# Own tile for the squares of Q, and the head's projections in another order, in a fused attention and mixing kernel

## Chip, cores and metric

The kernel runs as one program on all 8 cores of a Trainium2 chip. Each core works on two of the 16 sequences, and nothing is exchanged between cores. The metric is the device time of the slowest core, in microseconds (us); a median of runs is given. The profile shows one execution on its slowest core, core 4.

## What is computed

For every sequence x of 2048 tokens by 2048 features:

```
x = x + attn(layernorm(x)) @ Wo
x = x + layernorm(x) @ (sum of 8 factors / sqrt(8)) + bias

attn:  q = rmsnorm(h @ Wqa) @ Wqb          16 heads, each 128 (nope) + 64 (rope)
       ckv, k_pe = split(h @ Wkva)         512 + 64, k_pe shared by all heads
       k_nope, v = rmsnorm(ckv) @ Wkvb     16 heads, each 128 + 128
       rope on q_pe and k_pe
       softmax(causal(q k^T / sqrt(192))) v, per head
```

The softmax here isn't shifted by the true maximum of a row but by a bound on it, the product of the norm of the row's q and the largest norm of a k. For that bound the kernel needs, for every head, the squares of Q and K, the maximum of K's squares and the sums of Q's squares per token.

## The kernel before

A core treats its two sequences one after the other (`_emit_seq`). In each there are these stages: layer norm and the two low-rank projections by tiles of 128 tokens; the rope part of q for all heads; the 16 heads; the output projection with the second layer norm; the mixing matrix. The change lies in the heads, and there in what stands between two of them.

All engines have an order written out by hand: the program emits instructions engine by engine in the order of the Python code, each with the semaphores it waits for (`waits`) and the one that it raises (`inc`). ACT, DVE and the DMA queues go through theirs in that order.

A head's body is a loop over 16 tiles of keys. PE multiplies K with Q into psB (L897, and L902 for the 64 rope rows with two rows of statistics added), ACT takes the exponential (L914), DVE masks the diagonal (L921), PE multiplies with V into psA (L934) and sums the columns with small matmuls against a column of ones (L948). In between, ACT scales the next head's weights. When the body has ended, DVE copies psA out (L957) and takes the reciprocal of the sums (L963), which PE transposes (L966) and two small DMAs lay flat.

Between two heads three things follow:

- `prep` projects the next head in 16 groups of matmuls, each into one of six banks (psA 0 to 3, psB 2 and 3, in turn), and each followed by its eviction. `bn_group` makes Q (12 matmuls of 512 columns a group, L661; ACT evicts to QnT, L668), `c1_group` makes K (4 of 512, L678; ACT evicts to KnT, L685), `c2_group` makes V (16 of 128 columns, L698; DVE evicts to Vh, L706), `tq_group` transposes the rope part of q (4, L717; DVE evicts to QpeT_aug, L723). A group waits for the eviction of the group that had its bank before.
- PE spreads the reciprocals over all partitions (L997 to L1017), and ACT copies them out in two halves (L1007, L1024).
- `emit_mhat` makes the bound for the next head. ACT squares K into sq_all (L769), DVE takes the maximum along the tokens (L773) and casts it (L776). ACT then squares Q into the same tile sq_all (L779) and the rope part into sq_pe (L783). PE sums K's maximum (L789, L793) and then Q's squares in 32 matmuls of one column (L803, L808), and L813 spreads the K part. ACT and DVE make the square root of the product (L797, L817 to L828). In the first head of a sequence DVE also makes the maximum of the shared rope key first (L760 to L766).

Then DVE scales the head's output (L1033), makes the two rows of statistics (L843, L846), PE transposes them (L850), and two DMAs of 4 KB put them under QpeT_aug (L856, L859), which L902 waits for.

In the first sequence GpSimd also adds up the eight factors beside the heads (`emit_f_build`), with transfers of 1 MB (L221 to L230).

The tiles of this stage lie one behind the other in SBUF; sq_all takes 4 KiB of each partition.

Of the kernel before, what the change touches and what calls it, by code (L numbers as in the profile page):

```python
# [10 lines left out]
BF16 = mybir.dt.bfloat16  # L11
AF = mybir.ActivationFunctionType
# [3 lines left out]
S = 2048  # L16
# [69 lines left out]
def build_nc():  # L86
# [39 lines left out]
    ones_col = sb("ones_col", [128, 1], BF16)  # L126
# [53 lines left out]
    c_mq = ch("mq"); c_mt = ch("mt"); c_mv = ch("mv"); c_sg = ch("sg")  # L180
# [5 lines left out]
    for fn in [  # L186
# [26 lines left out]
      waits=[(c_bld, 16)], inc=c_bias)  # L213
# [29 lines left out]
    def rsb(name, shape, dt):  # L243
        _uid[0] += 1
        return rctx[0].enter_context(
            nc.sbuf_tensor(f"{name}_u{_uid[0]}", shape, dt, side="right"))
# [7 lines left out]
    def _emit_seq(sq):  # L254
# [47 lines left out]
        for tt in range(NT):  # L302
# [36 lines left out]
              waits=lw, inc=c_ln1)  # L339
# [228 lines left out]
        stage_w = rsb("stage_w", [128, 1536], F32)  # L568
        sq_all = rsb("sq_all", [128, S], BF16)
        sq_pe = rsb("sq_pe", [64, S], BF16)  # L570
        kpesq = rsb("kpesq", [64, S], BF16)
        neg_mh = rsb("neg_mh", [128, 32], F32)
        stat_sa = rsb("stat_sa", [128, 32], F32)
# [78 lines left out]
        def prep(h, pb0, pb1):  # L652
# [5 lines left out]
            def bn_group(cci):  # L658
                def g(bps, boff, waits):
                    for kb in range(12):  # L660
                        E("tensor", lambda e, kb=kb, cci=cci, bps=bps, boff=boff: e.matmul(  # L661
                            out=bps[:, boff:boff + 512],
                            lhsT=wqbn_h[hb][:, kb * 128:(kb + 1) * 128],
                            rhs=qa_v()[:, kb, cci * 512:(cci + 1) * 512],
                            start=(kb == 0), stop=(kb == 11)),
                          waits=(waits if kb == 0 else []),
                          inc=(c_bn if kb == 11 else None))
                    E("scalar", lambda e, cci=cci, bps=bps, boff=boff: e.activation(  # L668
                        out=QnT[hb][:, cci * 512:(cci + 1) * 512],
                        in_=bps[:, boff:boff + 512], func=AF.Copy),  # L670
                      waits=[(c_bn, c_bn.n)], inc=c_bn_ev)
                    return (c_bn_ev, c_bn_ev.n)
                return g, [whf_mark]

            def c1_group(cci):
                def g(bps, boff, waits):
                    for kb in range(4):
                        E("tensor", lambda e, kb=kb, cci=cci, bps=bps, boff=boff: e.matmul(  # L678
                            out=bps[:, boff:boff + 512],
                            lhsT=wkvbk_h[hb][:, kb * 128:(kb + 1) * 128],  # L680
                            rhs=ckv_v()[:, kb, cci * 512:(cci + 1) * 512],
                            start=(kb == 0), stop=(kb == 3)),
                          waits=(waits if kb == 0 else []),
                          inc=(c_c1 if kb == 3 else None))
                    E("scalar", lambda e, cci=cci, bps=bps, boff=boff: e.activation(  # L685
                        out=KnT[hb][:, cci * 512:(cci + 1) * 512],
                        in_=bps[:, boff:boff + 512], func=AF.Copy),
                      waits=[(c_c1, c_c1.n)], inc=c_c1_ev)
                    return (c_c1_ev, c_c1_ev.n)
                return g, [whf_mark]  # L690
# [37 lines left out]
                return g, [qpe_mark]  # L728

            for cci in range(4):  # L730
                groups.append(bn_group(cci))
            for cci in range(4):
                groups.append(c1_group(cci))
            for gg in range(4):
                groups.append(c2_group(gg))
            for gg in range(4):
                groups.append(tq_group(gg))

            banks = [(psA, 0), (psA, 512), (psA, 1024), (psA, 1536),
                     (psB, 1024), (psB, 1536)]  # L740
# [15 lines left out]
        def emit_mhat(h, pm):  # L756
            hb = h % 2
            if kpesq_pending[0]:
                kpesq_pending[0] = False
                E("vector", lambda e: e.tensor_mul(  # L760
                    out=kpesq[0:64, :], in0=kpeT_aug[0:64, :], in1=kpeT_aug[0:64, :]),
                  waits=[(c_tkpe_ev, c_tkpe_ev.n)], inc=c_mv)
                E("vector", lambda e: e.reduce_max(
                    out=kmax[0:64, :], in_=kpesq[0:64, :], axis=AX.X),
                  waits=[(c_mv, c_mv.n)], inc=c_mv)
                E("vector", lambda e: e.tensor_copy(  # L766
                    out=kpemax_bf[:], in_=kmax[0:64, :]),
                  waits=[(c_mv, c_mv.n)], inc=c_mv)
            E("scalar", lambda e, hb=hb: e.activation(  # L769
                out=sq_all[:], in_=KnT[hb][:], func=AF.Square),  # L770
              waits=[(c_mq, c_mq.n), (c_c1_ev, c_c1_ev.n), (c_sc, c_sc.n)],
              inc=c_sc)
            E("vector", lambda e: e.reduce_max(  # L773
                out=kmax[:], in_=sq_all[:], axis=AX.X),
              waits=[(c_sc, c_sc.n), (c_mv, c_mv.n)], inc=c_mv)
            E("vector", lambda e: e.tensor_copy(out=kmax_bf[:], in_=kmax[:]),  # L776
              waits=[(c_mv, c_mv.n)], inc=c_mv)
            km_mark = c_mv.n
            E("scalar", lambda e, hb=hb: e.activation(  # L779
                out=sq_all[:], in_=QnT[hb][:], func=AF.Square),  # L780
              waits=[(c_mv, km_mark), (c_bn_ev, c_bn_ev.n), (c_sc, c_sc.n)],
              inc=c_sc)
            E("scalar", lambda e, hb=hb: e.activation(  # L783
                out=sq_pe[0:64, :], in_=QpeT_aug[hb][0:64, :], func=AF.Square),
              waits=[(c_tq_ev, c_tq_ev.n), (c_sc, c_sc.n)], inc=c_sc)
            qsq_mark = c_sc.n
            smw = [(c_mv, km_mark)] + list(pm[0:2]) + \
                [(c_sdone, c_sdone.n)] + list(bank3_marks)
            E("tensor", lambda e: e.matmul(  # L789
                out=psB[0:1, 1700:1701], lhsT=kmax_bf[:], rhs=ones_col[:],  # L790
                start=True, stop=False),
              waits=smw)
            E("tensor", lambda e: e.matmul(  # L793
                out=psB[0:1, 1700:1701], lhsT=kpemax_bf[:], rhs=ones_col[0:64, :],
                start=False, stop=True),
              inc=c_mt)
            E("scalar", lambda e: e.activation(  # L797
                out=lnmk[:], in_=psB[0:1, 1700:1701], func=AF.Ln,
                scale=SCALE * SCALE * 1.05),
              waits=[(c_mt, c_mt.n)], inc=c_sc)  # L800
            lnmk_mark = c_sc.n
            for qt in range(NT):
                E("tensor", lambda e, qt=qt: e.matmul(  # L803
                    out=psB[:, 1040 + qt:1041 + qt],
                    lhsT=sq_all[:, qt * 128:(qt + 1) * 128], rhs=ones_col[:],
                    start=True, stop=False),
                  waits=([(c_sc, qsq_mark)] if qt == 0 else []))
                E("tensor", lambda e, qt=qt: e.matmul(  # L808
                    out=psB[:, 1040 + qt:1041 + qt],
                    lhsT=sq_pe[0:64, qt * 128:(qt + 1) * 128], rhs=ones_col[0:64, :],  # L810
                    start=False, stop=True),
                  inc=(c_mq if qt == NT - 1 else None))
            E("tensor", lambda e: e.matmul(  # L813
                out=psB[:, 1704:1705], lhsT=halfs1[:], rhs=lnmk[:],
                start=True, stop=True),
              waits=[(c_sc, lnmk_mark)], inc=c_mt)
            E("vector", lambda e: e.tensor_copy(out=lnmk_col[:], in_=psB[:, 1704:1705]),  # L817
              waits=[(c_mt, c_mt.n)], inc=c_mv)
            lc_mark = c_mv.n
            E("scalar", lambda e, hb=hb: e.activation(  # L820
                out=neg_mh[:, hb * 16:(hb + 1) * 16], in_=psB[:, 1040:1056], func=AF.Ln),
              waits=[(c_mq, c_mq.n)], inc=c_sc)
            E("scalar", lambda e, hb=hb: e.activation(
                out=neg_mh[:, hb * 16:(hb + 1) * 16],
                in_=neg_mh[:, hb * 16:(hb + 1) * 16], func=AF.Exp, scale=0.5,
                bias=lnmk_col[:]),
              waits=[(c_sc, c_sc.n), (c_mv, lc_mark)], inc=c_sc)
            E("vector", lambda e, hb=hb: e.tensor_scalar(  # L828
                out=neg_mh[:, hb * 16:(hb + 1) * 16],
                in0=neg_mh[:, hb * 16:(hb + 1) * 16], scalar1=-1.0,  # L830
                scalar2=None, op0=ALU.mult),
              waits=[(c_sc, c_sc.n)], inc=c_mv)
            return (c_mv, c_mv.n)
# [547 lines left out]
```

How the kernel before makes its waits and increments, by code:

```python
        def run(engine):  # L69
            for h, v in wl:
                engine.wait_ge(h, v)
            ins = fn(engine)
            if ih is not None:
                ins.then_inc(ih, amt)
# [5 lines left out]
        def run(engine):  # L80
            for h, v in wl:
                engine.wait_ge(h, v)
```

## Time and profile before

| | us |
|---|---|
| timed runs, median of 2 | 6312.1 (6295.76 and 6328.45) |
| the profiled execution | 6288.87 |
| its span, slowest core (core 4) | 6287.3 |
| spans of the other cores | 6264.1 to 6285.5 |
| mean granted clock of PE, by core | 0.761 to 0.766 |

The profiled execution is one more run beside the two. Its span goes from the first to the last instruction of the slowest core. The granted clock is a share of TensorE's full speed (2.4 GHz): a stretch shows 0.50 or 1.00, or a mean of these. Engines are PE (TensorE matmul), PEld (its weight loads), DVE (VectorE), ACT (ScalarE), POOL (GpSimd) and SP (SyncE). A matmul's record is longer than its share of the time where matmuls overlap.

### The profile page before, as it was taken

What the parts mean: (1) busy time and instruction counts of PE and PEld (TensorE: products, weight loads), DVE (VectorE), ACT (ScalarE), POOL (GpSimd) and SP (SyncE); (2) the same over time, 40 slices, a digit from 0 to 9 for tenths busy, and PEclk for the clock granted to TensorE, in tenths of its full rate; (3) what the DMA queues carried; (4) which work ended last, traced back from release to release, by engine and by line L of the source; (5) the groups of instructions that cost most, each with busy time, mean ns of one, the idle gap of its engine ahead of it and who ended that gap; (6) DMA issues with size and microseconds to landing.
All of it is one profiled execution on the core that took longest, in us unless ns stands there. A gap on an engine that the chain in (4) does not pass through costs nothing.

```text
span 6287.3 us, 67560 instructions; the slowest of 8 cores (6264.1 to 6287.3 us)
## 1 busy us (share of the span) xinstructions
PE 3942.4 (63%) x23520; PEld 1847.1 (29%) x23520; DVE 1099.3 (17%) x1945; ACT 1908.6 (30%) x3481; POOL 201.9 (3%) x284
## 2 busy tenths in 40 slices
PE   3665556666666663976636664666766666559666
PEld 1332222332333331432213231333333333224222
DVE  1222311111112110110002222212112111101000
ACT  1322033334343441530003331243443444235100
POOL 1000000000000000000010000000000000000000
PEclk8777777777777786988867776877777877689777
DMA  5001336676676305442250003100000000154422
GB/s 97 27 34 19 46 67 137 139 144 135 143 143 133 67 16 140 158 173 88 101 122 34 34 21 32 41 20 26 25 23 23 25 23 23 44 169 154 151 100 90
DMA packets 299615, 500.56 MB, mean 80 GB/s; under 512 B 141345, under 2 KB 227617, under 8 KB 262433
## 3 DMA queue, kind: packets, MB, share of 16 engines
q0 software_dynamic: 86400, 191.38, 17.0%
q1 hardware_dynamic: 189090, 220.57, 11.4%
q10 hardware_dynamic: 23808, 84.29, 3.5%
q8 instruction: 210, 3.44, 0.2%
q14 instruction: 107, 0.88, 0.1%
HBM read 418.59 MB, written 117.44 MB: 85 GB/s over the span
## 4 chain that ended last, share of the span: by engine, by line
PE 55%; ACT 14%; DMA 12%; issue 9%; DVE 5%; another core or an unknown queue 3%; SPq 1%; ACTq 1%; DVEq 0%; POOLq 0%
PE psA L661 6%; PE psA L385 6%; PE psA L934 5%; PE psB L1260 4%; DMA ln2T_u<-ln2t_s 4%; PE psA L1135 4%; PE psA L1260 4%; PE psB L1135 4%; PE psB L902 3%; PE psB L897 3%; ACT ptpool L914 3%; PE psA L511 3%; DMA stage_w_u<-wkvb 3%; PE psB L385 2%
## 5 line engine op out<-in xcount | busy, mean ns | idle before, releaser
L914 ACT ACTIVATE ptpool<-psB 128x512 bf16<-128x512 f32 (+3 forms) x1280 | 630.2, 532 | 820.8 <-PE psB L902 807.1
L934 PE MATMUL psA<-ptpool,Vh_u 128*128 128x512 bf16 (+3 forms) x1280 | 450.4, 394 | 336.5 <-DVE ptpool L921 205.6
L902 PE MATMUL psB<-QpeTa_u,kpeT_aug 66*128 66x512 bf16 (+3 forms) x1280 | 516.9, 404 | 121.1 <-DMA QpeTa_u<-sb_st 121.1
L385 PE MATMUL psA<-wa_bf,ln1T_u 128*128 128x512 bf16 x1536 | 472.8, 422 | 63.2 <-DVE ln1T_u L358 47.5
L897 PE MATMUL psB<-QnT_u,KnT_u 128*128 128x512 bf16 (+3 forms) x1280 | 495.3, 398 | 0.3
L661 PE MATMUL psA<-qa_nT,wqbnh_u 128*128 128x512 bf16 x1536 | 396.5, 426 | 37.6 <-ACT wkvbvh_u L638 37.6
L921 DVE TENSOR_TENSOR ptpool<-ptpool,maskT 128x128 bf16<-128x128 bf16 x512 | 115.6, 226 | 1455.2 <-ACT ptpool L914 1455.2
L1260 PE MATMUL psA<-f_bf_u,ln2T_u 128*128 128x512 bf16 x1024 | 260.7, 420 | 151.1 <-DMA ln2T_u<-ln2t_s 133.4
L1135 PE MATMUL psA<-wo_bf_u,OT_wo_u 128*128 128x512 bf16 x1024 | 233.2, 390 | 191.3 <-DMA wo_bf_u<-wo 179.6
L1260 PE MATMUL psB<-f_bf_u,ln2T_u 128*128 128x512 bf16 x1024 | 256.4, 417 | 149.6 <-DMA ln2T_u<-ln2t_s 149.6
L934 PEld LDWEIGHTS psA<-ptpool,Vh_u 128*128 128x128 bf16 x1280 | 128.9, 101 | 737.2 <-issue 722.5
L511 PE MATMUL psA<-wqbpe_bf,qa_nT 128*128 128x512 bf16 x768 | 170.0, 385 | 162.7 <-ACT wqbpe_bf L495 162.7
L352 PE MATMUL psB<-ident,ln_bf_u 128*128 128x128 bf16 x512 | 69.8, 303 | 281.4 <-ACT ln_bf_u L336 259.5
L661 PEld LDWEIGHTS psA<-qa_nT,wqbnh_u 128*128 128x128 bf16 x1536 | 162.4, 108 | 268.7 <-issue 129.3
L1135 PE MATMUL psB<-wo_bf_u,OT_wo_u 128*128 128x512 bf16 x1024 | 225.3, 381 | 12.0 <-ACT ln2ts_u L1108 12.0
L393 ACT ACTIVATE ptpool<-psB 128x512 bf16<-128x512 f32 x32 | 19.1, 597 | 703.8 <-PE psB L385 703.8
L385 PE MATMUL psB<-wa_bf,ln1T_u 128*128 128x512 bf16 (+1 forms) x1024 | 228.4, 307 | 0.0
L668 ACT ACTIVATE QnT_u<-psA 128x512 bf16<-128x512 f32 x128 | 76.5, 597 | 463.6 <-PE psA L661 463.6
L948 PEld LDWEIGHTS psB<-ones_col,ptpool 128*128 128x128 bf16 x4352 | 193.1, 100 | 79.3 <-issue 40.3
L308 ACT ACTIVATE ptpool<-xs_u 128x2048 bf16<-128x2048 f32 x32 | 60.6, 1894 | 491.6 <-DMA xs_u<-x 491.5
L1260 PEld LDWEIGHTS psA<-f_bf_u,ln2T_u 128*128 128x128 bf16 x1024 | 106.6, 106 | 305.8 <-issue 211.3
L1135 PEld LDWEIGHTS psA<-wo_bf_u,OT_wo_u 128*128 128x128 bf16 x1024 | 101.4, 100 | 319.5 <-issue 208.1
(161 smaller groups left out, 4675.9 us busy)
## 6 DMA issues: line engine op xcount, KB each, us to landing
acc_f<-fac POOLq DMA_DIRECT2D x128, 1024.0 KB, 8.5
xs_u<-x SPq DMA_DIRECT2D x32, 1024.0 KB, 4.8
xre_u<-x SPq DMA_DIRECT2D x32, 1024.0 KB, 6.8
r_s<-r1sb_u ACTq DMA_DIRECT2D x32, 1024.0 KB, 4.0
r1f_u<-r_s SPq DMA_DIRECT2D x32, 1024.0 KB, 7.1
out<-outsb_u SPq DMA_DIRECT2D x32, 1024.0 KB, 4.8
stage_w_u<-wqb SPq DMA_DIRECT2D x32, 768.0 KB, 5.7
stage_w_u<-wkvb SPq DMA_DIRECT2D x64, 256.0 KB, 3.2
```

Source lines behind the costliest of these rows:

```text
L385: E("tensor", lambda e, ti=ti, kb=kb, dst=dst, do=do, wdt=wdt, woff=woff: e.matmul(out=dst[:, do:do + wdt], lhsT=ln1T[ti][:, kb * 128:(kb ...
L511: E("tensor", lambda e, tt=tt, kb=kb, cci=cci, base=base: e.matmul(out=psA[:, base + cci * 512:base + (cci + 1) * 512], lhsT=qa_v()[:, kb, ...
L661: E("tensor", lambda e, kb=kb, cci=cci, bps=bps, boff=boff: e.matmul(out=bps[:, boff:boff + 512], lhsT=wqbn_h[hb][:, kb * 128:(kb + 1) * 128],
L668: E("scalar", lambda e, cci=cci, bps=bps, boff=boff: e.activation(out=QnT[hb][:, cci * 512:(cci + 1) * 512], in_=bps[:, boff:boff + 512], ...
L897: E("tensor", lambda e, hb=hb, kt=kt, q0=q0, wd=wd, boff=boff: e.matmul(out=psB[:, boff:boff + wd], lhsT=KnT[hb][:, kt * 128:(kt + 1) * 12 ...
L902: E("tensor", lambda e, hb=hb, kt=kt, q0=q0, wd=wd, boff=boff: e.matmul(out=psB[:, boff:boff + wd], lhsT=kpeT_aug[:, kt * 128:(kt + 1) * 128],
L914: E("scalar", lambda e, q0=q0, wd=wd, boff=boff, pto=pto: e.activation(out=ptpool[:, pto + q0:pto + q0 + wd], in_=psB[:, boff:boff + wd], ...
L921: E("vector", lambda e, qmin=qmin, pto=pto: e.tensor_tensor(out=ptpool[:, pto + qmin:pto + qmin + 128], in0=ptpool[:, pto + qmin:pto + qmi ...
L934: E("tensor", lambda e, hb=hb, kt=kt, q0=q0, wd=wd, pto=pto: e.matmul(out=psA[:, q0:q0 + wd], lhsT=Vh[hb][:, kt * 128:(kt + 1) * 128], rhs ...
L948: E("tensor", lambda e, kt=kt, qt=qt, pto=pto: e.matmul(out=psB[:, 1536 + qt:1537 + qt], lhsT=ptpool[:, pto + qt * 128:pto + (qt + 1) * 12 ...
L1135: E("tensor", lambda e, tt=tt, hh=hh, cci=cci, ps=ps: e.matmul(out=ps[:, cci * 512:(cci + 1) * 512], lhsT=OT_wo[:, hh * 2048 + tt * 128:hh ...
L1260: E("tensor", lambda e, kb=kb, cci=cci, bi=bi, ps=ps: e.matmul(out=ps[:, cci * 512:(cci + 1) * 512], lhsT=ln2T[bi][:, kb * 128:(kb + 1) * ...
```

## The change

Three things change: there is a new tile sq_q of the size of sq_all, which takes Q's squares; the waits of the two squares follow from that; and `prep` appends its groups in the order K, Q, rope part, V.

```diff
@@ -568,6 +568,7 @@
         sq_all = rsb("sq_all", [128, S], BF16)
         sq_pe = rsb("sq_pe", [64, S], BF16)
+        sq_q = rsb("sq_q", [128, S], BF16)
@@ -728,13 +729,13 @@
             for cci in range(4):
+                groups.append(c1_group(cci))
+            for cci in range(4):
                 groups.append(bn_group(cci))
-            for cci in range(4):
-                groups.append(c1_group(cci))
+            for gg in range(4):
+                groups.append(tq_group(gg))
             for gg in range(4):
                 groups.append(c2_group(gg))
-            for gg in range(4):
-                groups.append(tq_group(gg))
@@ -768,7 +769,7 @@
             E("scalar", lambda e, hb=hb: e.activation(
                 out=sq_all[:], in_=KnT[hb][:], func=AF.Square),
-              waits=[(c_mq, c_mq.n), (c_c1_ev, c_c1_ev.n), (c_sc, c_sc.n)],
+              waits=[(c_mv, c_mv.n), (c_c1_ev, c_c1_ev.n), (c_sc, c_sc.n)],
               inc=c_sc)
@@ -777,8 +778,8 @@
             E("scalar", lambda e, hb=hb: e.activation(
-                out=sq_all[:], in_=QnT[hb][:], func=AF.Square),
-              waits=[(c_mv, km_mark), (c_bn_ev, c_bn_ev.n), (c_sc, c_sc.n)],
+                out=sq_q[:], in_=QnT[hb][:], func=AF.Square),
+              waits=[(c_mq, c_mq.n), (c_bn_ev, c_bn_ev.n), (c_sc, c_sc.n)],
               inc=c_sc)
@@ -802,7 +803,7 @@
                 E("tensor", lambda e, qt=qt: e.matmul(
                     out=psB[:, 1040 + qt:1041 + qt],
-                    lhsT=sq_all[:, qt * 128:(qt + 1) * 128], rhs=ones_col[:],
+                    lhsT=sq_q[:, qt * 128:(qt + 1) * 128], rhs=ones_col[:],
                     start=True, stop=False),
```

The semaphore mq is raised by PE's last reduction of Q's squares (L808), mv by DVE's maxima, casts and norm, c1_ev, bn_ev, c2_ev and tq_ev by the evictions, scroll by each of ACT's passes here. From the new line on, line numbers of the changed kernel are higher by one.

On PE, from the transpose of the reciprocals (identf) to their first spreading (ones1, printed as ones), between two heads. Before:

```order
L966 MATMUL psB<-identf,invcol_u 16x128
L661 MATMUL psA<-qa_nT,wqbnh_u 128x512 x48
L678 MATMUL psB<-ckv_nT,wkvbkh_u 128x512 x8
L678 MATMUL psA<-ckv_nT,wkvbkh_u 128x512 x8
L698 MATMUL psA<-wkvbvh_u,ckv_nT 128x128 x32
L698 MATMUL psB<-wkvbvh_u,ckv_nT 128x128 x32
L717 MATMUL psA<-ident,qpesl_u 64x128 x16
L997 MATMUL psB<-invflat_u,ones 128x512
```

The same place on PE after the change:

```order
L967 MATMUL psB<-identf,invcol_u 16x128
L679 MATMUL psA<-ckv_nT,wkvbkh_u 128x512 x16
L662 MATMUL psB<-qa_nT,wqbnh_u 128x512 x24
L662 MATMUL psA<-qa_nT,wqbnh_u 128x512 x24
L718 MATMUL psA<-ident,qpesl_u 64x128 x8
L718 MATMUL psB<-ident,qpesl_u 64x128 x8
L699 MATMUL psA<-wkvbvh_u,ckv_nT 128x128 x64
L998 MATMUL psB<-invflat_u,ones 128x512
```

The same 144 matmuls stand between the same two neighbours; K comes to the front, V to the end, and the groups change banks.

On ACT, from the evictions to the logarithm behind the squares, at the same place, with the semaphores waited for. Before:

```order
L668 ACTIVATE QnT_u<-psA 128x512 [waits bn] x4
L685 ACTIVATE KnT_u<-psB 128x512 [waits c1] x2
L685 ACTIVATE KnT_u<-psA 128x512 [waits c1] x2
L1007 ACTIVATE invb_u<-psB 128x1024 [waits sg,scroll]
L1024 ACTIVATE invb_u<-psB 128x1024 [waits sg,scroll]
L769 ACTIVATE sq_all_u<-KnT_u 128x2048 [waits mq,c1_ev,scroll]
L779 ACTIVATE sq_all_u<-QnT_u 128x2048 [waits mv,bn_ev,scroll]
L783 ACTIVATE sq_pe_u<-QpeTa_u 64x2048 [waits tq_ev,scroll]
L797 ACTIVATE lnmk_u<-psB 1x1 [waits mt]
```

The same place on ACT after the change:

```order
L686 ACTIVATE KnT_u<-psA 128x512 [waits c1] x4
L669 ACTIVATE QnT_u<-psB 128x512 [waits bn] x2
L669 ACTIVATE QnT_u<-psA 128x512 [waits bn] x2
L1008 ACTIVATE invb_u<-psB 128x1024 [waits sg,scroll]
L1025 ACTIVATE invb_u<-psB 128x1024 [waits sg,scroll]
L770 ACTIVATE sq_all_u<-KnT_u 128x2048 [waits mv,c1_ev,scroll]
L780 ACTIVATE sq_q_u<-QnT_u 128x2048 [waits mq,bn_ev,scroll]
L784 ACTIVATE sq_pe_u<-QpeTa_u 64x2048 [waits tq_ev,scroll]
L798 ACTIVATE lnmk_u<-psB 1x1 [waits mt]
```

The evictions have changed places; the squares stand where they stood, behind the two copies of the broadcast, and mv and mq have changed places in their waits.

On DVE, in the first head of a sequence, from the evictions to the cast of K's maximum. Before:

```order
L706 CAST Vh_u<-psA 128x512 [waits c2] x2
L706 CAST Vh_u<-psB 128x512 [waits c2] x2
L723 CAST QpeTa_u<-psA 64x512 [waits tq] x4
L760 TENSOR_TENSOR kpesq_u<-kpeT_aug 64x2048 [waits tkpe_ev]
L763 TENSOR_REDUCE kmax_u<-kpesq_u 64x1 [waits mv]
L766 CAST kpemax_bf_u<-kmax_u 64x1 [waits mv]
L773 TENSOR_REDUCE kmax_u<-sq_all_u 128x1 [waits scroll,mv]
L776 CAST kmax_bf_u<-kmax_u 128x1 [waits mv]
```

The same place on DVE after the change:

```order
L724 CAST QpeTa_u<-psA 64x512 [waits tq] x2
L724 CAST QpeTa_u<-psB 64x512 [waits tq] x2
L707 CAST Vh_u<-psA 128x512 [waits c2] x4
L761 TENSOR_TENSOR kpesq_u<-kpeT_aug 64x2048 [waits tkpe_ev]
L764 TENSOR_REDUCE kmax_u<-kpesq_u 64x1 [waits mv]
L767 CAST kpemax_bf_u<-kmax_u 64x1 [waits mv]
L774 TENSOR_REDUCE kmax_u<-sq_all_u 128x1 [waits scroll,mv]
L777 CAST kmax_bf_u<-kmax_u 128x1 [waits mv]
```

The rope part's evictions come before V's; the three instructions for the shared rope key stay behind both, and K's squares on ACT now wait for the last of them.

## Rows read from the trace of the kernel before

**Rows 1.** The page: busy time (share) and instructions; and one costly group.

```profile
PE 3942.4 (63%) x23520; PEld 1847.1 (29%) x23520; DVE 1099.3 (17%) x1945; ACT 1908.6 (30%) x3481; POOL 201.9 (3%) x284
...
L668 ACT ACTIVATE QnT_u<-psA 128x512 bf16<-128x512 f32 x128 | 76.5, 597 | 463.6 <-PE psA L661 463.6
```

**Rows 2.** Chain that ended last, between two heads: start us, us, what.

```profile
4175.04 13.18 PE psA L661 x48
...
4195.24 1.01 PE psA L717 x16
...
4199.71 1.03 ACT invb_u L1024
4200.82 1.92 ACT sq_all_u L769
4202.90 2.30 DVE kmax_u L773
...
4209.71 0.16 PE psB L803
```

**Rows 3.** Same place in order of time: start us, us, instruction [idle before <-releaser].

```profile
4205.65 1.91 ACT L779 ACTIVATE sq_all_u<-QnT_u 128x2048 bf16<-128x2048 bf16 x1 [2.92 <-DVE kmax_bf_u L776]
4207.65 1.91 ACT L783 ACTIVATE sq_pe_u<-QpeTa_u 64x2048 bf16<-64x2048 bf16 x1
...
4206.23 0.16 PE L789 MATMUL psB<-ones_col,kmax_bf_u 128*1 128x1 bf16 x1 [6.67 <-DVE kmax_bf_u L776]
4206.32 0.16 PE L793 MATMUL psB<-ones_col,kpemax_bf_u 64*1 64x1 bf16 x1
4209.71 0.16 PE L803 MATMUL psB<-ones_col,sq_all_u 128*128 128x1 bf16 x1 [3.22 <-ACT lnmk_u L797]
```

**Rows 4.** Who waited for whom: us in total, times, longest us.

```profile
ACT sq_all_u L779 <- DVE kmax_bf_u L776: 110.0, 32, 10.6
```

**Rows 5.** In order of time, first head of the first sequence: ACT, DVE, PE.

```profile
817.52 1.91 ACT L769 ACTIVATE sq_all_u<-KnT_u 128x2048 bf16<-128x2048 bf16 x1
817.68 0.69 DVE L706 CAST Vh_u<-psA 128x512 bf16<-128x512 f32 x1 [35.04 <-PE psA L698]
...
820.97 2.47 DVE L723 CAST QpeTa_u<-psA 64x512 bf16<-64x512 f32 x4
...
827.05 0.15 DVE L766 CAST kpemax_bf_u<-kmax_u 64x1 bf16<-64x1 f32 x1
...
830.05 1.91 ACT L779 ACTIVATE sq_all_u<-QnT_u 128x2048 bf16<-128x2048 bf16 x1 [10.62 <-DVE kmax_bf_u L776]
...
834.11 0.16 PE L803 MATMUL psB<-ones_col,sq_all_u 128*128 128x1 bf16 x1 [3.54 <-ACT lnmk_u L797]
```

**Rows 6.** Stretches of 12 heads (first sequence) and 15 (second): length, busy, PEclk, DMA.

```profile
885.70:2102.20 1216.50, 770.50 (x5352) 368.63 (x5352) 211.19 (x445) 462.63 (x912) 114.48 (x144) 0.72 0.69 139
...
4077.60:5458.40 1380.80, 937.49 (x6690) 457.25 (x6690) 263.77 (x555) 572.97 (x1120) 0.00 (x0) 0.76 0.08 23
```

**Rows 7.** Short stretches, same columns: PE, PEld, DVE, ACT, POOL busy, PEclk, DMA, GB/s.

```profile
4199.60:4202.90 3.30, 0.00 (x0) 0.00 (x0) 0.00 (x0) 2.93 (x2) 0.00 (x0) 0.71 0.00 0
4202.90:4206.20 3.30, 0.00 (x0) 0.00 (x0) 2.44 (x2) 0.55 (x1) 0.00 (x0) 0.50 0.00 0
4209.70:4213.50 3.80, 3.79 (x33) 3.34 (x33) 0.00 (x0) 0.00 (x0) 0.00 (x0) 0.50 0.02 4
4225.20:4225.80 0.60, 0.60 (x19) 0.52 (x18) 0.00 (x0) 0.00 (x0) 0.00 (x0) 1.00 0.00 0
4216.80:4262.80 46.00, 33.76 (x257) 14.59 (x257) 4.25 (x20) 25.39 (x60) 0.00 (x0) 0.83 0.11 30
4122.20:4171.80 49.60, 37.28 (x257) 15.40 (x257) 4.23 (x20) 25.59 (x60) 0.00 (x0) 0.74 0.10 27
```

**Rows 8.** In order of time: first use of the statistics, two heads.

```profile
940.08 0.58 PE L902 MATMUL psB<-QpeTa_u,kpeT_aug 66*128 66x512 bf16 x1 [7.76 <-DMA QpeTa_u<-sb_st]
...
4220.90 0.58 PE L902 MATMUL psB<-QpeTa_u,kpeT_aug 66*128 66x512 bf16 x1 [2.46 <-DMA QpeTa_u<-sb_st]
```

**Rows 9.** In order of time: 16 matmuls of one column in a head's body.

```profile
4225.21 0.54 PE L948 MATMUL psB<-ones_col,ptpool 128*128 128x1 bf16 x16
```

## Prediction

> **What bounds the kernel now.** I read the page's busy line first, then the chain that ended last around one change of heads, then the order of time on the engines there, then the table of waits. PE carries most work but is busy for 63% of the span [rows 1], so what counts is where it stands still. The change touches only the stretch between two heads, 32 times in the program: 16 heads of two sequences, of which the first head of each follows other code. The chain through one such stretch [rows 2] reads as a single thread without slack: PE runs the projections of the next head back to back (from 4175.04 to about 4196), ACT copies the broadcast twice, squares K (L769, 1.92 us), DVE takes its maximum (L773, 2.30 us) and casts it (L776), and only then does ACT square Q (L779). ACT stands idle for 2.92 us before L779, with DVE's cast as releaser [rows 3]; over the program that wait is 110.0 us in 32 pieces [rows 4], and PE waits 3.22 us in front of the reductions L803 that follow [rows 3]. After L803 the thread goes on through the norm, the statistics' transpose and a small DMA to the first matmul that needs it (L902 [rows 8]). The next head starts only then, so a microsecond taken out of the thread is a microsecond of the head.
>
> **Part 1: a tile of its own for Q's squares.** Before, Q's squares overwrite the tile of K's squares, so L779 must wait for the maximum. Now they go to sq_q; L779 waits for the previous head's reductions (long done) and the evictions of Q (0.60 us each [rows 1], the last one done some 0.9 us after its matmuls). ACT then goes straight from K's squares to Q's, with the 0.09 us it shows between L779's end (4207.56) and L783's start [rows 3]. For the head of [rows 2, 3]: K's squares end at 4200.82 + 1.91 = 4202.73; Q's then run 4202.82 to 4204.73, the rope part's (L783) 4204.82 to 4206.73. L803 started 0.15 after L783's end (4209.56 to 4209.71), so now at 4206.88: 2.83 us earlier. The other path into L803 is PE's own queue: L789 needs the cast of the maximum, which does not move, and L793 ends at 4206.32 + 0.16 = 4206.48, so 0.4 us before. That path is what is late next.
> For the count I take the whole table: 110.0 us less the two first heads' waits of 10.62 us [rows 5] is 88.8 us in 30 pieces, 2.96 each; 0.09 stays, so 2.87 x 30 = 86.1 us. The tile costs 4 KiB a partition and no instruction.
>
> **Part 2: the order of the projections.** Before: Q (48 matmuls), K (16), V (64 small), rope part of Q (16). Now: K, Q, rope part, V. The instructions and their durations are the same. PE goes through them without a gap (48 matmuls in 13.18 us, then on to the last group at 4195.24 [rows 2]); in the new order each bank's former tenant is evicted in time: the first V group wants the bank of Q's third group, whose eviction by ACT takes 0.60 us, with a whole Q group and the rope part in between. ACT's queue is in order, and K's squares stand behind both broadcast copies there, whatever the order of evictions. So between heads the reordering alone brings nothing: I cost it at 0. Its cover is PE's queue; if one group stalled for one eviction, the price would be 0.6 us x 30 = 18 us, and on the other side nothing can be won, since PE's row is full. V's evictions are now the last on DVE; K's maximum is queued behind them there, but DVE stands idle for over 4 us before it, and the first user of V is in the next head's body, over 20 us later.
>
> **Part 3: the other waits.** K's squares now wait for DVE's last maximum or norm instead of the previous reductions. Between heads that is the norm's reciprocal, over 20 us old: 0. In the first head of a sequence it is the cast that ends the rope key's maximum (L766), and that is late: DVE ended its rope casts at 823.44 and the cast behind the key's maximum at 827.20 [rows 5]. Now K's squares start at 827.3 at the latest instead of 817.52, Q's follow to 831.2, the rope part's to 833.2, L803 at 833.4 instead of 834.11: 0.7 us won. Behind that wait in ACT's queue stand only the other squares and the norm, for which PE waits anyway. That is the low end, 1.4 for both sequences. Before, DVE's eight evictions ran one behind the other from 817.68 to 823.44, 5.8 us; in the new order they begin earlier, with the small rope part, and the last is one V cast of 0.69 us behind PE's end, so they can end up to a microsecond sooner: 1.7 each. I take 1.5 x 2 = 3 us, between 1.4 and 3.4.
>
> **What is given back.** In the first sequence GpSimd loads the factors beside the heads, 144 issues in its first 1216.5 us. Twelve heads fall there, 1216.5 / 12 = 101.4 us each; in the second sequence fifteen take 1380.8 / 15 = 92.1 us [rows 6]. The loads are paced by their own transfers, so they keep their 1.2 ms; with heads of 98.5 us about 0.35 head more falls under them, at 9.3 us: 3 us lost. Nothing later waits for them earlier.
>
> **Sum.** 86.1 + 3 - 3 = 86 us. The profiled execution took 6288.87 us (span 6287.3 and 1.6 around it): 6202.9. The two timed runs were 6295.76 and 6328.45; 6288.87 is the lowest of the three, and the middle one less 86 is 6210, which I predict, 1.4 to 1.6% under the runs.
>
> **The unknown: where the clock changes.** PE's granted clock falls to 0.50 in the idle stretch before L789 and is at 0.50 through L803 [rows 7], the 1.2 GHz level. In the head's body it comes back at a moment that differs: one body of 257 matmuls took 46.0 us at a mean clock of 0.83, the one before it 49.6 us at 0.74 [rows 7]. My change shifts every head's phase by 2.9 us, so I can't say which bodies will be the long ones. If all 32 went from the middle (47.8) to one end it would be 1.8 x 32 = 58 us either way; they mix, so I allow half, 29 us.
>
> **Rivals.**
> Gain held back under the factor loads. There the small DMA that ends the thread lands behind 1 MB transfers: PE waited 7.76 us for it in one head against 2.46 in a quiet one [rows 8]. If the 12 heads there only wait longer for the same transfer, their 12 x 2.87 = 34 us are lost: 6210 + 34 = 6244. For it: the wait is long there. Against it: the transfers run through the thread all the time, and nothing ties a head's end to one of them.
>
> The clock stays up. PE's idle stretch of 3.22 us before L803 [rows 3] all but vanishes. If with that the clock were at 2.4 GHz through the 33 small matmuls, their 3.8 us [rows 7] would shrink to about 1.1, at the 0.54 us for 16 that L948 shows where 1.00 is granted [rows 7, 9]: 2.7 x 30 = 81 us more, 6129. Against it: the clock has already fallen in the 6.67 us before L789 [rows 3], and that stretch is untouched. The Trainium skill ("TensorE: Matmul & The Clock Gate", section "Why this matters for your kernels") warns that an idle gap between bursts of matmuls brings the lower clock back; by that rule removing a gap is worth more than its length. The trace agrees that gaps lower the clock, but puts the fall into the gap that stays.
>
> The reordering does what its order suggests. If K's squares and maximum ran during Q's projections, the two squares left would follow L1024 at once: Q's at 4200.82, L803 at 4204.88, 4.83 x 30 = 145 us, about 6151. Against it: K's squares are issued behind L1024 on ACT and start 0.09 us after it.
>
> Slower: the passes get in each other's way. K's maximum on DVE and Q's squares on ACT now run side by side, on tiles of 2048 columns. The path over the maximum has 0.4 us of slack plus the 2.83 us won; it decides from a maximum of 2.3 + 3.2 = 5.5 us on. At three times its time (6.9 us) L803 would start 1.35 us later than before, 30 x 1.35 = 41 us: 6296 + 41 = 6337. Against it: K's squares took 1.91 us in the first head too, beside DVE's casts [rows 5], as between heads, where DVE stands idle.
>
> **Chances and range.** Forecast 80%; held back 10%; clock 5%; reordering 2%; slower 3%. The range reaches from 6288.9 - 86 - 29 = 6174 to the upper run's 6328.5 - 86 + 29 = 6271, rounded to 6270; it holds the held-back rival and leaves out the other three. A change over 2%, about what a measurement of this kernel can tell from none, means under 6186 from the median of 6312.1: the clock and reordering rivals, and a 5% tail of the forecast, 12%. Over 2% slower: 1%. Within: 87%.
>
> **What would show it.** Right: L779's wait on the cast gone from the table, Q's squares 0.09 us behind K's, PE's wait before the Q reductions down from 3.2 us to some 0.4, the 33 small matmuls still 3.8 us, PE gapless through the projections, the first head's K squares after the key's cast. Wrong: a gap in the projections, a longer maximum or longer squares, a wait for the small DMA that grows as the thread shortens, or a clock above 0.5 at L803.

## The result and the profile after

| us | before | after |
|---|---|---|
| median of all runs | 6360.0 (18 runs) | 6290.0 (19 runs) |
| lowest run | 6284.2 | 6211.6 |
| ratio of undisturbed runs | 1 | 0.9907 [0.9864, 0.9950] |
| profiled execution | 6288.87 | 6219.97 |
| span in it: slowest core, mean of the eight | 6287.3, 6276.5 | 6218.4, 6190.7 |
| undisturbed dies: mean of their cores | 6278.3 (25 dies) | 6193.5 (25 dies) |
| undisturbed dies: their slowest core | 6290.5 | 6209.4 |

In about half of the executions of either kernel the cores of one die, or of both, run at a lower granted clock and take longer (in the profile of e5, below, core 4 shows 0.81 from 730 to 828 us); the medians hold these executions, the ratio leaves them out, and the last two rows count only dies whose cores show a mean granted clock of 0.76 or more, from all runs of the two kernels whose cores are listed, before's first profile apart.

The change took 84.8 us from the mean core (6278.3 to 6193.5, standard errors 1.3 and 2.2), and the forecast of the saving was 86. On the slowest core, which is the metric, the saving came out smaller: 81.1 us between the slowest cores of a die (6290.5 to 6209.4), 68.9 in the profiled executions, 70.0 between the medians, and some 58 by the ratio, with an interval of 31 to 86. The median, 6290.0, lies above the range that I gave, 6174 to 6270. Most of that is the level from which the saving was taken: before itself, run 18 times, has a median of 6360.0, while I had two timed runs and a profiled one, the lowest two of which were 6288.9 and 6295.8.

The page of after, its span and its busy line:

```profile
span 6218.4 us, 67560 instructions; the slowest of 8 cores (6134.0 to 6218.4 us)
...
PE 3957.3 (64%) x23520; PEld 1847.6 (30%) x23520; DVE 1093.4 (18%) x1945; ACT 1909.3 (31%) x3481; POOL 201.3 (3%) x284
```

No engine does much less than in [rows 1]: PE 3957 against 3942 us, ACT 1909 against 1909, DVE 1093 against 1099. The time came out of idle stretches. The chain that ended last, between two heads of the second sequence (start, us, what):

```profile
4145.14 5.55 PE psA L679 x16
4150.69 5.18 PE psB L662 x24
4155.87 5.18 PE psA L662 x24
4161.05 0.56 PE psA L718 x8
4161.61 0.45 PE psB L718 x8
4162.06 3.68 PE psA L699 x64
...
4169.19 1.03 ACT invb_u L1025
4170.31 1.92 ACT sq_all_u L770
4172.31 1.92 ACT sq_q_u L780
4174.31 1.71 ACT sq_pe_u L784
```

PE's row through the projections has no hole: each piece begins where the last one ended, in the new order K, Q, rope part, V. Behind the copy L1025 the chain now stays on ACT for three squares. The maximum and its cast, which stood between the first two in [rows 2], are off it. In order of time, with the idle time before each and its releaser:

```profile
4172.31 1.91 ACT L780 ACTIVATE sq_q_u<-QnT_u 128x2048 bf16<-128x2048 bf16 x1
4172.39 2.29 DVE L774 TENSOR_REDUCE kmax_u<-sq_all_u 128x1 f32<-128x2048 bf16 x1 [5.85 <-ACT sq_all_u L770]
4174.31 1.91 ACT L784 ACTIVATE sq_pe_u<-QpeTa_u 64x2048 bf16<-64x2048 bf16 x1
4175.72 0.16 PE L790 MATMUL psB<-ones_col,kmax_bf_u 128*1 128x1 bf16 x1 [6.67 <-DVE kmax_bf_u L777]
...
4176.37 0.16 PE L804 MATMUL psB<-ones_col,sq_q_u 128*128 128x1 bf16 x1 [0.40 <-ACT lnmk_u L798]
```

L780 has no idle time before it, where L779 had 2.92 us [rows 3], and L804 has 0.40 where L803 had 3.22. From the start of the second copy to the first reduction it was 10.00 us (4199.71 to 4209.71, [rows 2]) and is 7.18 (4169.19 to 4176.37): 2.82 less, and the prediction worked out 2.83. The table of waits, whole program, says the same of all heads; L779's wait of 110.0 us [rows 4] has become its last line here, 0.4 us:

```profile
ACT sq_all_u L770 <- DVE kpemax_bf_u L767: 17.5, 2, 8.8
...
PE psB L804 <- ACT lnmk_u L798: 11.8, 29, 0.7
...
ACT sq_q_u L780 <- ACT sq_all_u L770: 0.4, 1, 0.4
```

The first line is the wait that the changed semaphores add in the two first heads. Short stretches of after, with the columns of [rows 7]:

```profile
4169.90:4173.20 3.30, 0.00 (x0) 0.00 (x0) 0.81 (x1) 3.12 (x3) 0.00 (x0) 0.50 0.00 0
4176.30:4180.20 3.90, 3.83 (x33) 3.38 (x33) 0.00 (x0) 0.00 (x0) 0.00 (x0) 0.50 0.02 4
```

The 33 small matmuls still take 3.8 us at 0.50.

**Where the core's time went, stage by stage.** I cut the two profiled executions by the order of time on DVE: a head's body goes from its statistics cast (L843 before, L844 after) to the copy of psA that ends it (L957, L958), and a gap from there to the next statistics cast. Means over the eight cores:

| us | before | after | difference |
|---|---|---|---|
| up to the first statistics cast | 836.3 | 833.4 | -2.9 |
| 15 gaps, first sequence | 662.9 | 620.5 | -42.4 |
| 13 bodies, most beside the factor loads | 730.8 | 742.7 | +11.9 |
| 3 bodies behind them | 141.3 | 143.4 | +2.1 |
| between the sequences' heads | 1653.0 | 1641.1 | -11.9 |
| 15 gaps, second sequence | 663.1 | 622.6 | -40.5 |
| 16 bodies, second sequence | 760.3 | 761.1 | +0.8 |
| from the last body to the end | 828.9 | 826.0 | -2.9 |
| span | 6276.5 | 6190.7 | -85.8 |

The 30 gaps give 82.9 us, 2.76 each. The bodies beside the loads lose 11.9 and the stretch between the sequences is shorter by the same on the mean, so that together the two rows are 2383.8 in both kernels. Core by core they don't make up for each other: core 0 gained in both (28.9 and 31.1), and core 5 lost 30.0 in its bodies and got 2.0 back. The slowest core did worse than the mean: its span fell by 68.9, since the cores lie further apart. The 13 bodies, core by core (0 to 7):

| | |
|---|---|
| before | 736.0 733.1 730.9 730.6 732.6 728.5 722.3 732.3 |
| after | 707.1 754.3 749.1 729.5 751.3 758.5 755.1 736.7 |

### The profile page after: what moved, and what is told of

Read it like the earlier page. It is cut to its first block, busy times and chain, and to the rows that moved or that the text cites. A ratio compares the mean times of both kernels' runs of the same rounds, so it can differ in the third digit from the quotient of the medians.

```text
span 6218.4 us, 67560 instructions; the slowest of 8 cores (6134.0 to 6218.4 us)
## 1 busy us (share of the span) xinstructions
PE 3957.3 (64%) x23520; PEld 1847.6 (30%) x23520; DVE 1093.4 (18%) x1945; ACT 1909.3 (31%) x3481; POOL 201.3 (3%) x284
## 4 chain that ended last, share of the span: by engine, by line
PE 55%; ACT 15%; DMA 12%; issue 8%; DVE 4%; another core or an unknown queue 3%; SPq 1%; ACTq 1%; DVEq 0%; POOLq 0%
PE psA L385 6%; PE psA L935 5%; PE psB L1261 4%; PE psA L1261 4%; PE psA L1136 4%; DMA ln2T_u<-ln2t_s 4%; PE psB L1136 4%; PE psB L903 3%; PE psB L898 3%; ACT ptpool L915 3%; DMA stage_w_u<-wkvb 3%; PE psA L679 3%; PE psA L511 3%; PE psA L662 3%
## 5 line engine op out<-in xcount | busy, mean ns | idle before, releaser
L935 PEld LDWEIGHTS psA<-ptpool,Vh_u 128*128 128x128 bf16 x1280 | 129.2, 101 | 754.8 <-issue 739.6
L679 PE MATMUL psA<-ckv_nT,wkvbkh_u 128*128 128x512 bf16 x512 | 174.6, 517 | 37.4 <-ACT wkvbvh_u L639 37.4
L903 PEld LDWEIGHTS psB<-QpeTa_u,kpeT_aug 66*128 66x128 bf16 x1280 | 134.2, 105 | 210.0 <-issue 163.7
L1261 PEld LDWEIGHTS psB<-f_bf_u,ln2T_u 128*128 128x128 bf16 x1024 | 107.8, 106 | 298.7 <-issue 203.2
```

What stands on the lines that cost most here:

```text
L903: E("tensor", lambda e, hb=hb, kt=kt, q0=q0, wd=wd, boff=boff: e.matmul(out=psB[:, boff:boff + wd], lhsT=kpeT_aug[:, kt * 128:(kt + 1) * 128],
L935: E("tensor", lambda e, hb=hb, kt=kt, q0=q0, wd=wd, pto=pto: e.matmul(out=psA[:, q0:q0 + wd], lhsT=Vh[hb][:, kt * 128:(kt + 1) * 128], rhs ...
L1261: E("tensor", lambda e, kb=kb, cci=cci, bi=bi, ps=ps: e.matmul(out=ps[:, cci * 512:(cci + 1) * 512], lhsT=ln2T[bi][:, kb * 128:(kb + 1) * ...
```

## The experiments

Theory A: the whole gain is the 2.87 us of ACT's wait in each gap, and the order of the projections is worth nothing. Theory B: the order takes a part, or gives one back. Theory C: what falls beside the factor loads is held back there by the transfers. The ratios are to before, with 95% intervals; "dies" are means over undisturbed dies, as above.

### The tile alone, and the order alone

`e1_tile_only` is after with the old order of the groups, `e2_order_only` is before with the new one:

```diff
             for cci in range(4):
-                groups.append(c1_group(cci))
-            for cci in range(4):
                 groups.append(bn_group(cci))
-            for gg in range(4):
-                groups.append(tq_group(gg))
+            for cci in range(4):
+                groups.append(c1_group(cci))
             for gg in range(4):
                 groups.append(c2_group(gg))
+            for gg in range(4):
+                groups.append(tq_group(gg))
```

> The tile for Q's squares and the waits as in the changed kernel, the projections in the old order. Sums over a sequence's 15 gaps between heads (from the copy of psA to the first statistics cast), mean of the 8 cores: 662.9 and 663.1 us before, 620.5 and 622.6 with the change. Theory: the tile alone makes the whole gain in the gaps, 2.7 to 2.9 us each, so 620 to 623 us a sequence, and the 13 bodies beside the factor loads (730.8 us before, 742.7 after, spread over the cores from 707 to 759 after) come out anywhere from 725 to 760. Rival, the order works too: gaps stay above 630 us, because part of the gain was the order's. Rival, the order lengthens the bodies beside the loads: without it all cores return to 722 to 736 us.

> The projections in the new order, Q's squares still in K's tile with the old waits. Theory: no gain between heads: gap sums stay at 661 to 665 us a sequence, ratio 0.995 to 1.005. Rival, the order works too: gap sums below 655 us. Rival, the order lengthens the bodies beside the factor loads: 13 bodies at 743 to 760 us on most cores with the gaps unchanged, ratio 1.002 to 1.005.

Measured: the tile alone 0.9837 [0.9745, 0.9928], dies 6191.9 (8 dies), gaps 620.0 and 619.1. The order alone 0.9967 [0.9931, 1.0003], dies 6278.1 (17), gaps 665.2 and 663.5. So the tile alone takes 86.4 us from a core and the order alone 0.2, with a standard error of 3 and 2. The waits of the order alone are those of before [rows 4]:

```profile
ACT sq_all_u L779 <- DVE kmax_bf_u L776: 108.0, 32, 9.6
...
PE psB L803 <- ACT lnmk_u L797: 103.7, 32, 3.5
```

Theory A holds, and B falls to within these errors. The bodies beside the loads, 734.9 and 722.8, stand on either side of before's 730.8; over the cores their standard deviation is 11.1 with the tile alone and 4.0 with the order alone, against 3.8 in before.

### Without most of the factor loads

Seven of the eight factors are left out, in before (`e3_before_1fac`) and in after (`e4_after_1fac`), so that for each block of rows GpSimd issues one load of 1 MB and the store of 512 KB, instead of eight such loads and the store:

```diff
-            for r in range(1, 8):
+            for r in range(1, 1):
```

> The kernel before with one factor loaded instead of the sum of eight (seven of the eight factors are left out of the mixing matrix), so the factor transfers end after about two heads instead of thirteen. Theory: gap sums as before (661 to 665 us a sequence); the bodies of the first sequence fall from 56 us beside the loads to the 47.5 us of the second sequence, so about 11 x 8.7 = 95 us less in all, some 6190 us. Rival, the long bodies have another cause than the loads: the first sequence stays near 872 us for its 16 bodies.

> The changed kernel with one factor loaded instead of the sum of eight (seven of the eight factors are left out). Theory: with the loads gone nothing is given back: gaps 620 to 623 us a sequence, bodies equal to those of the kernel before with one factor within 8 us, and the whole is 83 to 90 us below that kernel (ratio to it 0.985 to 0.988). Rival, the bodies grow because of the change itself and not of the loads: its bodies in the first sequence are 12 us or more above those of the other, and the difference is 60 to 70 us.

Measured: before 0.9839 [0.9732, 0.9947], dies 6179.7 (7 dies); after 0.9675 [0.9617, 0.9732], dies 6095.3 (7). The change takes 84.4 us from a core without these loads and 84.8 with them; the loads cost 98.6 us before and 98.2 after. So on the whole core no loss of the gain shows, against C; but the difference between 84.4 and 84.8 has a standard error of 6, and a loss of some 10 us can't be excluded. The profiled execution of e3 took 6536.2 us, so its stages aren't compared; in e4 the gaps took 618.7 and 622.2 us (forecast 620 to 623), and the stretch between the sequences 1651.3, where after had 1641.1. What the loads do to the bodies is plain in the waits of after's slowest core, in 850 to 2200 us:

```profile
PE psB L903 <- DMA QpeTa_u<-sb_st: 78.3, 13, 8.5
...
ACT wkvbkh_u L626 <- DMA stage_w_u<-wkvb: 43.8, 12, 6.0
...
ACT wkvbvh_u L639 <- DMA stage_w_u<-wkvb: 38.1, 11, 6.3
```

and in the same stretch of after's slowest core with one factor:

```profile
PE psB L903 <- DMA QpeTa_u<-sb_st: 51.8, 15, 7.4
...
ACT wkvbkh_u L626 <- DMA stage_w_u<-wkvb: 2.8, 1, 2.8
...
ACT wkvbvh_u L639 <- DMA stage_w_u<-wkvb: 2.6, 2, 2.3
```

Behind the big transfers PE waits longer for the 4 KB of statistics, and ACT waits for the next head's weights, 82 us against 5. Over the cores of after the sum of the three waits goes with the 13 bodies: 126 us where the bodies took 707 (core 0, the fastest), 160 where they took 758 (core 5, the slowest). The waits, 34 of these 51 us, aren't all of it: the granted clock of that stretch is 0.75 on core 0 and 0.73 on core 5. How long the transfers took from issue to landing (median, last number) is in the same stretch of the same two profiles, after's first:

```profile
stage_w_u<-wkvb SPq DMA_DIRECT2D x28, 256.0 KB, 7.5
...
QpeTa_u<-sb_st ACTq DMA_DIRECT2D x26, 4.0 KB, 5.9
```

```profile
stage_w_u<-wkvb SPq DMA_DIRECT2D x30, 256.0 KB, 3.1
...
QpeTa_u<-sb_st ACTq DMA_DIRECT2D x30, 4.0 KB, 1.8
```

The same waits tell which of them grew with the change. On the mean of the eight cores, from 850 to 2200 us, PE's wait for the statistics went from 80.1 us before to 76.7 after, and ACT's for the next head's weights from 55.7 to 69.2. So the wait that grew is the one for the weights, and not the one for the small transfer at the end of the thread; its 13.5 us are about what the 13 bodies lost (11.9).

### The loads at another phase

`e5_loads_earlier` is after with the factor work beginning behind 20 exponentials instead of 40, so that it meets each head at another point:

```diff
-        p.wait("gpsimd", [(c_pt, 40)])
+        p.wait("gpsimd", [(c_pt, 20)])
```

> The changed kernel, with the factor transfers let go after 20 instead of 40 exponentials of the first head, some 20 us earlier. Theory: how the heads fall against the transfers decides how long the 13 bodies beside them take, by the waits for the small DMA and for the staged weights; so the gaps stay at 620 to 623 us a sequence, the 13 bodies scatter over the cores again (standard deviation 8 us or more, mean anywhere from 715 to 760) and other cores are the long ones than in the changed kernel (there cores 0 and 3 were the short ones, 707 and 730). Rival, the shorter gap itself costs the bodies 12 us: mean of 740 to 746 again with the same cores short.

There is no ratio for it. Its undisturbed dies give 6199.7 (5 dies, standard error 4.7), against after's 6193.5: no difference beyond the error. In its profile the 13 bodies of cores 0 to 3 took 754.8, 739.9, 720.3 and 752.4 us, where after had 707.1, 754.3, 749.1 and 729.5. Other cores are long now. But after itself, run once more (`e9_after_again`, below), has 744.5, 726.4, 738.6 and 715.4 on the same four cores, so e5 can't tell the moved loads from the scatter of two executions of one program.

### Both kernels once more

`e9_after_again` and `e10_before_again` are the two kernels as they are, on another chip.

> The changed kernel once more, for a second profiled execution. Theory: the gaps come out the same to 2 us a sequence (620 and 623), the second sequence's bodies to 4 us (761), and the 13 bodies beside the factor loads scatter over the cores again, 705 to 760 us, with other cores short than 0 and 3; where a core's waits for the small DMA and the staged weights sum to 126 us its bodies take some 707, at 160 us some 758. Rival, the phase is fixed by the program: the same cores come out at the same bodies to 8 us.

> The kernel before once more, for a second profiled execution. Theory: gaps 663 us a sequence, bodies beside the loads 722 to 736 us as in the first profile if its narrow scatter belongs to the kernel, wider if it was luck; waits for the small DMA and the staged weights 130 to 144 us a core. Rival to the theory that the long bodies of the changed kernel are chance: the kernel before stays at 731 with a scatter of 4, the changed one at 743 with 16.

Measured: 6215.39 for after, mean core 6189.3, gaps 622.2 and 620.8, 13 bodies 739.2 on the mean, standard deviation 13.0 over the cores. Cores 0 to 3 came out 10 to 37 us away from the first time, cores 4 to 7 within 5 us (748.9, 757.0, 750.8 and 731.8), so the rival held for cores 4 to 7 and fell for cores 0 to 3. The waits again go with the bodies: 120 us on core 3, which took 715.4, and 156 on core 5, which took 757.0. Before: 6325.06, gaps 665.2 and 664.1, bodies 728.1, standard deviation 4.2. So the longer and more scattered bodies of after come again (16.3 the first time, against 3.8), and so does the shorter stretch between the sequences (1644.0 against 1652.3). ACT's wait for the weights is again the one that differs, 66.0 us against 57.7 on the mean core, while PE's for the statistics is 76.5 against 76.0.

### The squares before the copies

The forecast had said that the new order is worth nothing as long as K's squares stand behind both copies in ACT's queue. Three versions of after issue them earlier. `e6_ksq_early` issues K's squares and maximum ahead of the spreading of the reciprocals, `e7_allsq_early` all three squares, and `e8_allsq_aug` besides makes the next head's statistics before DVE scales this head's output. The core of e7, and what e8 adds:

```diff
+            if h + 1 < NH:
+                km_mark = emit_ksq(h + 1)
+                qsq_mark = emit_qsq(h + 1)
             pm01 = [prep_marks[0]] if h + 1 < NH else []
...
             if h + 1 < NH:
-                mh_ready = emit_mhat(h + 1, prep_marks)
+                mh_ready = emit_mhat(h + 1, prep_marks, km_mark, qsq_mark)
...
+            if h + 1 < NH:
+                bank3_marks = [prep_marks[1], mh_ready]
+                st_ev_mark = augstats(h + 1, mh_ready)
+                bank3_marks = [st_ev_mark]
             E("vector", lambda e, h=h: e.tensor_mul(
```

> The changed kernel, with K's squares and their maximum issued right behind the evictions, ahead of the two copies of the broadcast on ACT. Theory: the new order of projections can now pay, since K's squares and maximum come off the thread; Q's squares follow the second copy at once, L804 comes 2.0 us sooner, gaps 620 - 30 = 590 and 592 us a sequence, the whole 55 to 62 us below the changed kernel. Rival, the first copy is held up by K's squares (1.91 us) as long as they save: gaps unchanged at 618 to 623.

> The changed kernel, with all three squares and K's maximum issued right behind the evictions, ahead of the copies of the broadcast on ACT. Theory: the copies come some 1.2 us later, but L804 follows the broadcast's last matmul: about 5.8 us less a gap, gaps near 620 - 87 = 533 us a sequence, the whole some 175 us below the changed kernel before what the bodies beside the loads give or take (20 us). Rival, ACT becomes the bound there, since the squares wait for the rope part's evictions and hold the copies: 2 to 4 us less a gap, gaps 560 to 590.

> The kernel before this one in the list, with the two rows of statistics made ahead of the scaling of the head's output on DVE (2.29 us), and their DMAs issued ahead of the output's. The gap as I count it ends at the first statistics cast, which then stands 2.2 us earlier: gaps 500 us a sequence if they were 533. Theory: the small DMA leaves 2.2 us sooner and the scaling runs under its flight, 66 us in all. Rival, the scaling now delays the next head's first mask on DVE, or the output's transfer the staged weights: the bodies get longer by as much, ratio within 0.003 of the kernel without it.

| us | ratio to before | dies | 15 gaps, each sequence | 13 bodies (sd) |
|---|---|---|---|---|
| e6 | 0.9722 [0.9680, 0.9764] | 6106.4 (7) | 591.9, 591.6 | 719.9 (7.2) |
| e7 | 0.9564 [0.9499, 0.9630] | 6002.4 (7) | 530.5, 529.7 | 731.6 (7.0) |
| e8 | 0.9488 [0.9381, 0.9594] | 5940.8 (8) | 500.7, 499.9 | 721.6 (12.1) |

The chain of e7 between two heads:

```profile
4138.98 5.20 PE psA L662 x24
4144.50 0.25 issue
4144.76 1.91 ACT sq_all_u L770
4146.75 1.92 ACT sq_q_u L783
4148.75 1.92 ACT sq_pe_u L787
4150.75 1.03 ACT invb_u L1019
...
4153.37 0.12 PE psB L810
```

The squares follow the last eviction of Q, while PE goes on with the rope part and V; before, the first of them began after both copies. In e8 a gap as counted takes 10.8 us less than before ((662.9 - 500.7) / 15), and e8 is the fastest version, 0.9488 of before. Against the version that each was compared with, the forecasts were 55 to 62 us for e6, some 175 give or take 20 for e7 and 66 for e8; measured on the dies were 87.1, 191.1 and 61.6. In e6 the gaps gave 59.6, as forecast, and the rest came from shorter bodies. The three versions also answer a question on the bodies: their gaps are shorter still than after's, yet their bodies beside the loads are no longer (719.9, 731.6, 721.6 against 742.7). A shorter gap does not as such lengthen them on the mean. It goes with their scatter: the standard deviation over the cores is 3.8 to 4.2 in the profiles with the old gap (both of before, and e2), and 7.0 to 16.3 with a shorter one (both of after, e1, e6, e7 and e8).

## Why the prediction was right, and where it was wrong

**The tile, 86.1 us: right.** Thirty gaps gave 82.9 us in the profile, 2.76 each for 2.87, and the mean core as a whole 84.8 over the dies counted above; alone, the tile gave 86.4. Q's squares begin 0.09 us after K's end, and the path over the maximum is late next by the 0.40 us forecast: PE waits 0.40 us before L804.

**The order, 0: right.** Alone it changed a core by 0.2 us.

**The first heads, 1.5 each: right in kind, somewhat small.** From the first projection to the first statistics cast the slowest cores' time went from 38.3 us (800.79 to 839.11) to 36.8 (795.97 to 832.75), 1.5 less. On the mean of the eight cores it was 1.9 less in the first sequence (38.5 to 36.6) and 2.1 in the second (38.6 to 36.4): 4.0 together, where the sum had 3 and at most 3.4. The squares of K wait 8.75 us for the rope key's cast there, and all that is queued behind them had waited longer before:

```profile
821.34 0.15 DVE L767 CAST kpemax_bf_u<-kmax_u 64x1 bf16<-64x1 f32 x1
...
821.69 1.91 ACT L770 ACTIVATE sq_all_u<-KnT_u 128x2048 bf16<-128x2048 bf16 x1 [8.75 <-DVE kpemax_bf_u L767]
823.69 1.91 ACT L780 ACTIVATE sq_q_u<-QnT_u 128x2048 bf16<-128x2048 bf16 x1
```

**The step that failed is the base of the sum and of the range.** The step reads "the middle one less 86 is 6210", and the range went "from 6288.9 - 86 - 29 = 6174 to the upper run's 6328.5 - 86 + 29 = 6271". Three executions stood for the level of all, and 29 us was the allowance for the clock, with none for how far the median of many runs can lie from these. It lies at 6360.0. Of the 80 us by which 6290.0 lies above 6210, 64 are this base (6360.0 against 6295.8) and 16 the saving (70.0 between the medians for 86). Whether the 16 is more than chance these medians can't tell: drawn again from the runs, their difference has a 95% interval of some 20 to 125 us. The lowest run took 6211.6, near the forecast. The two runs shown already differed by 33 us, more than the allowance, and that difference was the warning: the same kernel had an unknown of that size which had nothing to do with the change. With the range so narrow, 0.90 for the two cases inside it (forecast and held back) was too much. A slip besides: 6210 is 1.3 to 1.9% under the three executions, and not 1.4 to 1.6.

**What is given back, 3 us: mis-sized.** It counted more of a head under the loads and left the waits there as they were. The bodies beside the loads took 11.9 us more on the mean core and up to 30 on one (core 5: 728.5 to 758.5), and ACT's wait for the next head's weights, which the sum had at nothing, grew by 13.5. That the mean core still gained 85.8 for 86 in the profile is in part luck: the stretch between the sequences was shorter by 11.9, which no step forecast, and what shortens it stays open. A second term left at nothing was the scatter: the slowest core, which sets the profiled time, gained 68.9 where the mean gained 85.8. The scatter goes with the shorter gaps; why it is larger in after than in e6 to e8, and which cores will be the long ones, stays open.

**The clock, 29 us either way: not needed in the quiet heads.** The second sequence's bodies took 760.3 us and 761.1. There a shift of every head's phase by 2.8 us didn't choose long or short bodies.

**The rivals.** The clock stays up: fell, 0.50 through the small matmuls. The Trainium skill ("TensorE: Matmul & The Clock Gate", section "Why this matters for your kernels") holds that an idle gap between bursts brings the lower clock back; the trace agrees, since PE's idle stretch of 6.67 us before L790 is as long as in [rows 3] and the clock is at 0.50 behind it. The reordering does what its order suggests: fell here, but its working was right for the kernel that it assumed. It gave 4.83 us a gap, and e6, where K's squares do run during the projections, shows (662.9 - 591.9) / 15 = 4.73. Slower, the passes get in each other's way: fell, the maximum took 2.29 us beside Q's squares and the squares 1.91. Held back under the loads: its 34 us fell on the whole core (84.4 without the loads, 84.8 with, give or take 6), and the wait it named, for the small DMA, didn't grow (80.1 to 76.7 us). What the bodies lost went with the wait for the weights; no run tested that by itself.

The chance of 0.87 for "within 2%" was on the case that came.

## What to carry to other kernels

A buffer that one engine reuses while another still reads it shows as an idle stretch with the reader's last step as releaser; its worth is what of that wait goes (2.83 of 2.92 us), times its count, as long as the path that is late next has slack left (here 0.40 us), and here that came out at 84.8 us a core for 86. An instruction order on one engine is worth nothing while what it feeds is queued behind something later on the next engine: read that queue first, and move the squares too (e7, e8), which brought three times as much again. And give the level of a kernel and the size of a change separate ranges: here the size came out within 2 us on the mean core, while before's median of many runs lies 32 to 71 above the three executions shown. The slowest core needs an allowance of its own, since a change that scatters the cores gives it less than the mean.

## What the runs showed of the hardware

- Two cores that run the same program can differ by 50 us in 13 heads (707.1 and 758.5 in one execution of after), 34 us of it in waits for transfers of 4 KB and 256 KB beside 1 MB ones (126 and 160 us). With one factor of eight the cores of after agree (632.1, standard deviation 3.3).
- A transfer of 4 KB took 5.9 us from issue to landing (median) beside these loads and 1.8 with one factor of eight; one of 256 KB 7.5 and 3.1.
- A pass on ACT that depends on the pass just before it, or on a semaphore long raised, begins 0.09 us after that ends (4174.22 to 4174.31 above).
- A maximum on DVE and a square on ACT, both over 2048 columns and side by side, did not slow each other: 2.29 and 1.91 us, as when alone (2.30 and 1.91, [rows 2, 3]).
